# The attention-values product in four array quadrants, and one step order per engine, in a four-layer graph kernel

## The chip, the cores and the metric

The kernel runs on one core of one Trainium2 chip. The metric is the device time of one execution in microseconds (us), from launch to end. Five engines of the core take part, each with its own in-order instruction stream: PE (matrix multiplies, with PEld for the weight loads in front of them), DVE (vector engine), ACT (scalar engine), POOL (GpSimd) and SP (issues DMAs). They are kept in step by semaphores alone.

## The reference, cut to what matters

128 graphs of 64 nodes with 256 features pass four layers, each followed by a residual sum and a layer norm. The first layer is attention with 8 heads of 64; the change touches its last two products. The other three (mean aggregation, hypergraph convolution, gated similarity) matter as work that shares the engines.

```python
qkv = (x @ W_qkv).reshape(B, N, HEADS, 3, DIM_HEAD)
...
attn = jax.nn.softmax(dots, axis=-1) * LA
...
attn = attn + LG * adj + LD * jnp.exp(-dist)
out = jnp.einsum('bhij,bhjd->bhid', attn, v)
out = jnp.transpose(out, (0, 2, 1, 3)).reshape(B, N, HEADS * DIM_HEAD)
return out @ W_out + b_out
```

## The kernel before, in words

**Tiles and groups.** A tile is 128 rows, two graphs of 64 nodes. Four tiles (T) make a group, 16 groups (GRP) the whole input. Features are cut in 2 chunks of 128, the 512 inner columns in 4.

**Three groups in flight.** Line 305, `run`, walks one table, `SCHEDULE` (line 42), of (stream, step, index). Stream N is the next group (splitting its x in a high and a low part, its queries and first key chunk), A the group in layer 0, B the group before it in layers 1 to 3, C the group before that (its last scaling and its store). `rounds` (line 294) calls it for 19 rounds; 15 of them have both A and B, and 13 of these form the hardware loop. Every engine walks the same table and skips the steps it has no part in. So the table is the instruction order of PE, ACT, DVE and POOL alike. It also deals out the eight banks of PE's accumulation memory: lines 69 to 79 give banks 0 to 3 in turn to fills of N and A and banks 4 to 7 to those of B, in table order, and a fill waits (`emptied`, line 284) until the fill before it in its bank was read out.

**Precision.** Most products are three matmuls of a high and a low part (`product`, line 881). A step that feeds one is read out of its bank twice: by ACT, which writes the high part (`copy_out`, line 499), then by DVE, which writes what is left (`low_part`, line 598, the instruction at line 604). The next PE step waits for the low part.

**Scores** (`score`, line 938) are 64x64 products, one per head and graph, two tiles at a time. An instruction takes rows 0 to 63 or 64 to 127 of its operands, by the head's parity e, and writes partitions 0 to 63 or 64 to 127 of a bank, by the graph gr. Even heads write one bank and odd heads another. So four consecutive matmuls use the four combinations of input half and output half, called quadrants here.

**Values** (`pv`, line 973) take one tile per step. Head e = 0 or 1 of a pair is read from half e and written to half e of a single bank, so two of the four quadrants are used:

```python
for p in range(HP):
    for gr in range(2):
        for e in range(2):
            rows = slice(e * N, (e + 1) * N)
            ins = pe.matmul(dst[rows, p * P + gr * N:p * P + (gr + 1) * N], v[rows, i, gr, p, :],
                            pT[rows, i % 2, p, gr * N:(gr + 1) * N], start=True, stop=True,
```

ACT (line 522) and DVE (line 659) read that bank out into the parts of `oT`, which `out0` (line 995) multiplies with the output weights.

**Steps named below.** On PE: `q`, `k`, `v` projections (`proj`, 922; `val`, 931); `turnp` (964) transposes probabilities; `turn1`, `turn_h`, `turn3` (1003) transpose a layer's input; `graph_a` to `graph_d` and `graph_m` prepare the adjacency; `agg`, `spread`, `agg3` (`gathered`, 1058) apply it; `mean`, `up`, `down`, `hyper`, `qk`, `sim`, `out3` are products of layers 1 to 3. On DVE: `scale` (675, the instruction at 680) finishes a layer norm: `scale0`, `scale1`, `scale3`, and in `gated` (827), which also writes xg, the input of `turn3`. On POOL: `inv_root` (405) gives the factor that `scale` waits for; `residual` (396, step "mask") adds the bias to x; `split_low` (444) makes the low part of the next group's x. In this kernel `agg` waits for `turn1`'s low part, because it is given the bank that held it.

Of the kernel before, what the change touches and what calls it, by code (L numbers as in the profile page):

```python
# [13 lines left out]
ACT = mybir.ActivationFunctionType  # L14
# [6 lines left out]
P = 128  # L21
N = 64
D = 256
B = 128
H = 8
DH = 64
HID = 512
# [3 lines left out]
C = D // P  # L31
HP = H // 2
# [6 lines left out]

SCHEDULE = [
# [14 lines left out]
]  # L57

FILLS = {"graph_a": ["ht"], "graph_b": ["cnt"], "graph_c": ["sym"], "graph_m": ["meanT"], "graph_d": ["gT"],
# [6 lines left out]
_order = []  # L68
for _s, _n, _i in SCHEDULE:
    for _f in FILLS.get(_n, [_n]):  # L70
# [47 lines left out]
def graph_layers(nc, x, x_t, adj, adj_row0, mask_rows, wqkv, w_out, b_out, w_mean_t, w1_t, b1, gamma_c, beta_c, w2_t, b2,  # L118
                 wqk_t, bqk_c, wl_t, bl, wr_t, wd_r, bd_r, ident_c, ones3_c, mrow_c, out):
    with ExitStack() as ctx:  # L120
        def sb(name, shape, dt=F32):
            return ctx.enter_context(nc.sbuf_tensor(name, shape, dt))
# [47 lines left out]
        v = sb("v", [P, T, 2, HP, DH])  # L170
# [5 lines left out]
        pT = sb("pT", [P, 2, HP, P])  # L176
        oT = split("oT", [P, HP, 2 * P])
# [25 lines left out]
        agg3 = aggT  # L203
# [5 lines left out]
        gate = r[:, C:2 * C, :].rearrange("p a (b d) -> p (a b) d", d=D)  # L209
        xg = yw  # L210
        sim = hT0
# [45 lines left out]
        def count(sem, g, k, back=0):  # L257


            n = g * PER[sem] + (k - back * PER[sem])  # L260
            return (zero_ready, 4) if isinstance(n, int) and n <= 0 else (SEM[sem], n)

        def apart(eng, g):


            if not isinstance(g, int):
                eng.sem_inc(parted, 1)
# [7 lines left out]
        def bank_of(fill, i):  # L275
            return bank[BANK[(fill, i)][0]]
# [7 lines left out]
        def emptied(fill, i, g):  # L284

            b, (f, j), back = BEFORE[(fill, i)]
            if f in ("s_even", "s_odd"):
                return count("shift_ready", g, 2 * j + 1 + (f == "s_odd"), back)
            return count(READ_OUT[f], g, j + 1, back)

        def now_full(ins, fill, i):
            ins.then_inc(full[BANK[(fill, i)][0]], 1)

        def rounds(eng, body):

            body(0, None, None, None)
            body(1, 0, None, None)
            body(2, 1, 0, None)
            with eng.Fori(1, GRP - 2) as g:
                body(g + 2, g + 1, g, g - 1)  # L300
            body(None, GRP - 1, GRP - 2, GRP - 3)
            body(None, None, GRP - 1, GRP - 2)
            body(None, None, None, GRP - 1)

        def run(steps, n, a, b, c):
            group = {"N": n, "A": a, "B": b, "C": c}
            for stream, name, i in SCHEDULE:
                if group[stream] is not None and name in steps:
                    steps[name](group[stream], i)

# [77 lines left out]
        def _(pool):  # L388
# [80 lines left out]
                "out3": lambda g, i: inv_root(g, 3, "3", 2 * i, 2 * i + 2, i),  # L469
                "up": lambda g, i: inv_root(g, 4, "_h", i, i + 1, i),  # L470
            }
            rounds(pool, lambda n, a, b, c: run(steps, n, a, b, c))

        @block.scalar
        def _(act):
# [46 lines left out]
            def pv(g, i):  # L522
                act.wait_ge(*filled("oT", i, g))
                src = bank_of("oT", i)
                ins = act.activation(oT[0][:, :, (i % 2) * P:(i % 2 + 1) * P],  # L525
                                     src[:, :].rearrange("p (a n) -> p a n", a=HP), ACT.Copy)
                ins.then_inc(SEM["oT_hi"], 1)

            def graph_a(g, i):
# [31 lines left out]
                "turn_s": lambda g, i: copy_out(g, "turn_s", 0, flat(sT[:, :, :]), "sT_ready"),  # L561
                "agg3": lambda g, i: copy_out(g, "agg3", i, agg3[0][:, i, :], "agg3_hi"),
            }
            rounds(act, lambda n, a, b, c: run(steps, n, a, b, c))

        @block.vector
        def _(dve):
# [30 lines left out]
            def low_part(g, fill, i, lo, hi, name):  # L598

                dve.wait_ge(*count(f"{name}_hi", g, i + 1))  # L600
                src = bank_of(fill, i)[:, :]
                if len(lo.shape) == 3:
                    src = src.rearrange("p (a n) -> p a n", a=lo.shape[1])
                dve.tensor_tensor(lo, src, hi.bitcast(F32), ALU.subtract).then_inc(SEM[f"{name}_lo"], 1)  # L604
# [52 lines left out]
                    split_weight(wlr, raw_lr)  # L657

            def pv(g, i):
                at = slice((i % 2) * P, (i % 2 + 1) * P)  # L660
                low_part(g, "oT", i, oT[1][:, :, at], oT[0][:, :, at], "oT")
                if isinstance(g, int) and g == 0 and i < 2:
                    other_weights(i)

# [207 lines left out]
                "spread": low_chunk(spT, "spread", "spread"), "turn_h": low_chunk(hT, "turn_h", "hT"),  # L872
                "turn3": low_chunk(xgT, "turn3", "turn3"), "agg3": low_chunk(agg3, "agg3", "agg3"),
            }
            rounds(dve, lambda n, a, b, c: run(steps, n, a, b, c))

        @block.tensor
        def _(pe):
# [92 lines left out]
                now_full(ins, "pT", i)  # L971

            def pv(g, i):
                pe.wait_ge(*count("pT_ready", g, i + 1))
                pe.wait_ge(*count("v_ready", g, i + 1))
                pe.wait_ge(*emptied("oT", i, g))
                dst = bank_of("oT", i)
                apart(pe, g)
                for p in range(HP):
                    for gr in range(2):  # L980
                        for e in range(2):
                            rows = slice(e * N, (e + 1) * N)
                            ins = pe.matmul(dst[rows, p * P + gr * N:p * P + (gr + 1) * N], v[rows, i, gr, p, :],  # L983
                                            pT[rows, i % 2, p, gr * N:(gr + 1) * N], start=True, stop=True,
                                            skip_group_check=True)
                now_full(ins, "oT", i)

            def two_tiles(name, i, pairs_of, bias=None, ready=()):

# [163 lines left out]
                "turn3": lambda g, i: turned("turn3", g, i, xg, "xg_ready", 2),  # L1153
                "qk": qk, "sim": simi, "turn_s": turn_s, "agg3": agg3_, "out3": out3,
            }
            rounds(pe, lambda n, a, b, c: run(steps, n, a, b, c))


# [40 lines left out]
```

## Time and profile before

| | |
|---|---|
| device time, median of 3 runs | 1324.53 us (1323.3 to 1326.96) |
| profiled execution, device time | 1325.2 us |
| its span, first to last instruction | 1323.4 us |
| PE busy | 1238.9 us, 94% |
| DVE busy | 962.0 us, 73% |
| ACT, POOL busy | 551.2 us, 504.5 us |

The span is what the trace covers; 1.8 us of the execution lie outside it. "Busy" is the union of an engine's instruction records. A PE record lasts longer than the time after which the next can start, so several overlap: what a step costs is read from start to start, not from the length of a record. In the timeline a row gives start, length, instruction and count, and in brackets how long the engine was idle ahead of it and who ended that.

### The profile page before, as it was taken

How to read it: one execution, taken by the hardware profiler on the slowest of the kernel's cores; microseconds unless marked ns; L12 is line 12 of the kernel's file. 1: busy time of each engine (PE TensorE's matmuls, PEld its weight loads, DVE VectorE, ACT ScalarE, POOL GpSimd, SP SyncE). 2: the span in 40 equal slices, each digit the busy share in tenths (PEclk: the TensorE clock that was granted, in tenths of full speed). 3: DMA queues.
4: the chain of work that ended last, by engine and by line, in shares of the span. 5: the costliest groups of instructions: out<-in, count | busy, mean ns of one | idle time of the engine just before them, and what ended most of it. 6: DMA issues, size and time to landing. Idle time of an engine off the chain costs nothing.

```text
span 1323.4 us, 30705 instructions
## 1 busy us (share of the span) xinstructions
PE 1238.9 (94%) x11728; PEld 1073.7 (81%) x11728; DVE 962.0 (73%) x2115; ACT 551.2 (42%) x1058; POOL 504.5 (38%) x633
## 2 busy tenths in 40 slices
PE   5799999999999999999999999999999999999786
PEld 4688888788888888888788888878888887888665
DVE  5787776778767677776777777677876767787653
ACT  3335343543535344353444435354353435435221
POOL 2326252442624335262433525244262524425130
PEclk9799999999999999999999999999999999999897
DMA  6000101001010100101010010100101010010000
GB/s 204 21 21 17 42 2 41 16 20 36 0 54 2 40 16 20 36 0 44 12 40 16 20 36 0 40 16 20 36 16 40 0 40 20 0 37 2 21 1 16
DMA packets 43874, 34.93 MB, mean 26 GB/s; under 512 B 19320, under 2 KB 38718, under 8 KB 43839
## 3 DMA queue, kind: packets, MB, share of 16 engines
q1 hardware_dynamic: 43112, 34.04, 8.2%
q10 hardware_dynamic: 726, 0.40, 0.2%
q8 instruction: 24, 0.39, 0.1%
q14 instruction: 12, 0.09, 0.0%
HBM read 26.05 MB, written 8.39 MB: 26 GB/s over the span
## 4 chain that ended last, share of the span: by engine, by line
PE 72%; DVE 17%; issue 6%; ACT 3%; DMA 1%; POOL 0%; DVEq 0%; SPq 0%; POOLq 0%
PE bank L890 16%; PE bank L892 15%; PE bank L891 15%; PE bank L1066 6%; DVE x L680 5%; PE bank L1010 3%; PE bank L983 3%; PE bank L958 3%; DVE hT_lo L604 2%; PE bank L1124 2%; PE bank L886 2%; DVE yw L832 2%; DVE stats L669 1%; PE bank L948 1%; PE bank L1039 1%
## 5 line engine op out<-in xcount | busy, mean ns | idle before, releaser
L410 POOL TENSOR_SCALAR var<-mv 128x2 f32<-128x2 f32 (+1 forms) x192 | 43.4, 226 | 665.5 <-DVE mv L673 665.5
L680 DVE TENSOR_SCALAR x<-x,mv,rstd 128x256 f32<-128x256 f32 x256 | 158.3, 665 | 11.0 <-POOL rstd L413 11.0
L413 POOL TENSOR_TENSOR rstd<-var,negh 128x2 f32<-128x2 f32 (+1 forms) x192 | 130.4, 679 | 16.0
L502 ACT ACTIVATE qT<-bank 128x512 f32<-128x512 f32 x64 | 38.4, 600 | 217.9 <-PE bank L892 217.9
L604 DVE TENSOR_TENSOR hT_lo<-bank,hT_hi 128x512 fp32r<-128x512 f32 x160 | 105.3, 684 | 31.0 <-ACT hT_hi L502 30.7
L502 ACT ACTIVATE hT_hi<-bank 128x512 fp32r<-128x512 f32 x160 | 89.1, 604 | 52.8 <-PE bank L1066 46.0
L514 ACT ACTIVATE v<-bank 64x256 f32<-64x256 f32 x256 | 97.2, 380 | 17.5 <-PE bank L892 14.5
L669 DVE BATCH_NORM_STATS2 stats<-x 128x6 f32<-128x256 f32 x256 | 96.4, 419 | 4.4
L519 ACT ACTIVATE prob<-prob 128x512 f32<-128x512 f32 x64 | 40.5, 633 | 124.3 <-DVE prob L714 124.3
L525 ACT ACTIVATE oT_hi<-bank 128x512 fp32r<-128x512 f32 x64 | 38.2, 597 | 116.3 <-PE bank L983 116.3
L669 DVE BATCH_NORM_STATS2 stats<-r 128x6 f32<-128x512 f32 x64 | 44.4, 694 | 57.3 <-ACT r L502 57.3
L455 POOL TENSOR_TENSOR prob<-prob,srec 128x512 f32<-128x512 f32 x64 | 66.9, 1045 | 48.4 <-DVE srec L722 48.4
L460 POOL TENSOR_TENSOR prob<-prob,mix 128x512 f32<-128x512 f32 x64 | 82.2, 1285 | 6.1 <-POOL prob L455 2.1
L890 PE MATMUL bank<-w_hi,hT_hi 128*128 128x256 f32 x256 | 74.1, 289 | 0.2 <-DVE hT_lo L604 0.2
L890 PE MATMUL bank<-wo_hi,oT_hi 128*128 128x256 f32 x256 | 73.0, 285 | 0.5 <-DVE x L729 0.5
L890 PE MATMUL bank<-wm_hi,hT_hi 128*128 128x256 f32 x256 | 72.7, 284 | 0.0
L892 PE MATMUL bank<-wo_hi,oT_lo 128*128 128x256 f32 x256 | 71.5, 279 | 0.0
L891 PE MATMUL bank<-wo_lo,oT_hi 128*128 128x256 f32 x256 | 71.4, 279 | 0.0
L983 PEld LDWEIGHTS bank<-pT,v 64*64 64x64 f32 x2048 | 63.8, 137 | 9.4 <-issue 5.0
L892 PE MATMUL bank<-wm_hi,hT_lo 128*128 128x256 f32 x256 | 71.3, 279 | 0.0
L891 PE MATMUL bank<-wm_lo,hT_hi 128*128 128x256 f32 x256 | 71.3, 279 | 0.0
L891 PE MATMUL bank<-w_lo,hT_hi 128*128 128x256 f32 x256 | 71.1, 278 | 0.0
(206 smaller groups left out, 3864.1 us busy)
## 6 DMA issues: line engine op xcount, KB each, us to landing
xTin<-in_x_t SPq DMA_DIRECT2D x32, 256.0 KB, 2.8
xin<-in_x SPq DMA_DIRECT2D x16, 512.0 KB, 3.7
out_x<-x SPq DMA_DIRECT2D x32, 256.0 KB, 2.2
adjA<-in_adj SPq DMA_DIRECT2D x16, 128.0 KB, 2.5
adjB<-in_adj SPq DMA_DIRECT2D x32, 64.0 KB, 3.0
r<-in_wqkv SPq DMA_DIRECT2D x2, 512.0 KB, 8.9
x<-in_wqkv SPq DMA_DIRECT2D x1, 512.0 KB, 10.4
x<-in_w_out SPq DMA_DIRECT2D x1, 512.0 KB, 10.7
```

The lines of the kernel that those rows point to most:

```text
L413: pool.tensor_tensor(rstd[layer][:, lo:hi], var[layer][:, lo:hi], negh[:, lo:hi], ALU.pow).then_inc(SEM[f"rstd{n}"], 1)
L460: pool.tensor_tensor(u, u, mix[:, t:t + 2, :].rearrange("p t (a n) -> p t a n", a=1) .broadcast_to([P, 2, HP, N]), ALU.add).then_inc(SEM[" ...
L502: act.activation(dst, src[:, :], func, **kw).then_inc(SEM[ready], 1)
L514: ins = act.activation(v[e * N:(e + 1) * N, i, gr, :, :], src[gr * N:(gr + 1) * N, e], ACT.Copy)
L604: dve.tensor_tensor(lo, src, hi.bitcast(F32), ALU.subtract).then_inc(SEM[f"{name}_lo"], 1)
L669: dve.bn_stats(stats[layer][:, t, :], src[:, t, :]).then_inc(SEM[f"stats{n}"], 1)
L680: ins = dve.tensor_scalar(x[:, t, :], x[:, t, :], mv[layer][:, t, 0:1], rstd[layer][:, t:t + 1], ALU.subtract, ALU.mult)
L890: pe.matmul(out_ap, l[0], rr[0], start=(bias is None and j == 0), stop=False)
L891: pe.matmul(out_ap, l[0], rr[1], start=False, stop=False)
L892: ins = pe.matmul(out_ap, l[1], rr[0], start=False, stop=(j == len(pairs) - 1))
L983: ins = pe.matmul(dst[rows, p * P + gr * N:p * P + (gr + 1) * N], v[rows, i, gr, p, :], pT[rows, i % 2, p, gr * N:(gr + 1) * N], start=Tru ...
L1066: ins = pe.matmul(dst[:, t * P:(t + 1) * P], src[:, t, i * P:(i + 1) * P], mat[:, t, :], start=True, stop=True)
```

## The change

`pv` on PE does its work at even indices only, for two tiles i and i + 1 at once, and nothing at odd ones. Even head pairs (odd = 0) are written to halves e as before, in the bank of `oT` i. Odd head pairs (odd = 1) are written with the halves swapped, in the bank of `oT` i + 1. So a bank now holds half of the heads for both tiles; ACT and DVE write it to every second chunk of `oT`, and the output weights come with their rows permuted to fit. The number of matmuls stays. In place of the one table each engine walks its own order; the banks are dealt out by PE's. The stretches of the orders that matter are shown; between them steps stand much as before.

```diff
-SCHEDULE = [
-    ("A", "k", 1), ("B", "graph_a", 0), ("C", "scale3", 0), ("B", "turn1", 0), ("A", "mask", 0), ("B", "turn1", 1),
-    ("A", "k", 2), ("B", "graph_b", 0), ("B", "graph_m", 0), ("A", "k", 3), ("B", "agg", 0), ("A", "mixmat", 0),
-    ("B", "agg", 1), ("A", "score", 0), ("A", "shift", 0), ("B", "graph_c", 0), ("A", "shift", 1), ("B", "mean", 0),
-    ("B", "mean", 1), ("B", "graph_d", 0), ("A", "v", 0), ("B", "scale1", 0), ("A", "v", 1), ("A", "soft", 0),
...
-    ("A", "pv", 0), ("A", "pv", 1), ("B", "hyper", 1), ("A", "turnp", 2), ("A", "turnp", 3), ("B", "gated", 0),
-    ("A", "out0", 0), ("B", "gated", 1), ("N", "split_low", 0), ("N", "split", 0), ("A", "pv", 2), ("A", "pv", 3),
-    ("B", "turn3", 0), ("B", "turn3", 1), ("A", "norm0", 0), ("N", "q", 0), ("B", "qk", 0), ("B", "qk", 1),
...
+PE_ORDER = [
+    ("B", "turn1", 0), ("B", "turn1", 1), ("A", "k", 1), ("B", "graph_a", 0), ("A", "k", 2), ("B", "graph_m", 0),
+    ("B", "graph_b", 0), ("A", "k", 3), ("A", "mixmat", 0), ("B", "agg", 0), ("B", "agg", 1), ("B", "graph_c", 0),
+    ("A", "score", 0), ("B", "mean", 0), ("B", "mean", 1), ("B", "graph_d", 0), ("A", "v", 0), ("A", "v", 1),
+    ("A", "v", 2), ("B", "spread", 0), ("B", "spread", 1), ("A", "v", 3), ("B", "up", 0), ("B", "up", 1),
...
+    ("A", "score", 1), ("A", "turnp", 0), ("B", "down", 0), ("B", "down", 1), ("A", "turnp", 1), ("B", "hyper", 0),
+    ("A", "pv", 0), ("B", "hyper", 1), ("A", "turnp", 2), ("A", "turnp", 3), ("A", "pv", 1), ("A", "out0", 0),
+    ("A", "pv", 2), ("B", "turn3", 0), ("B", "turn3", 1), ("N", "q", 0), ("B", "qk", 0), ("A", "pv", 3),
...
+ACT_ORDER = [
+    ("B", "turn1", 0), ("B", "turn1", 1), ("A", "k", 1), ("B", "graph_a", 0), ("B", "graph_m", 0), ("A", "mixmat", 0),
+    ("A", "k", 2), ("B", "agg", 0), ("A", "k", 3), ("B", "agg", 1), ("A", "shift", 0), ("A", "v", 0),
+    ("B", "graph_d", 0), ("A", "v", 1), ("B", "spread", 0), ("B", "spread", 1), ("A", "shift", 1), ("N", "split", 0),
...
+DVE_ORDER = [
+    ("B", "graph_a", 0), ("B", "turn1", 0), ("B", "turn1", 1), ("A", "mask", 0), ("C", "scale3", 0),
+    ("B", "graph_b", 0), ("B", "agg", 0), ("B", "agg", 1), ("B", "graph_c", 0), ("A", "mixmat", 0), ("A", "shift", 0),
+    ("B", "mean", 0), ("B", "mean", 1), ("B", "scale1", 0), ("A", "shift", 1), ("B", "spread", 0), ("B", "spread", 1),
...
+POOL_ORDER = [
+    ("B", "graph_a", 0), ("B", "graph_b", 0), ("B", "mean", 0), ("A", "mask", 0), ("B", "mean", 1), ("A", "soft", 0),
...
+    ("A", "soft", 2), ("A", "soft", 3), ("N", "split_low", 0), ("B", "hyper", 0), ("B", "hyper", 1),
...
@@ ACT @@
-                ins = act.activation(oT[0][:, :, (i % 2) * P:(i % 2 + 1) * P],
-                                     src[:, :].rearrange("p (a n) -> p a n", a=HP), ACT.Copy)
+                ins = act.activation(oT[0][:, i % 2:HP:2, :], src[:, :].rearrange("p (a n) -> p a n", a=HP // 2), ACT.Copy)
@@ DVE @@
-                low_part(g, "oT", i, oT[1][:, :, at], oT[0][:, :, at], "oT")
+                low_part(g, "oT", i, oT[1][:, i % 2:HP:2, :], oT[0][:, i % 2:HP:2, :], "oT")
@@ PE @@
             def pv(g, i):
+                if i % 2:
+                    return
+                pe.wait_ge(*count("pT_ready", g, i + 2))
+                pe.wait_ge(*count("v_ready", g, i + 2))
+                for odd in range(2):
+                    pe.wait_ge(*emptied("oT", i + odd, g))
+                    apart(pe, g)
+                ins = [None, None]
+                for k in range(2):
+                    for pair in range(HP // 2):
+                        for gr in range(2):
+                            for odd in range(2):
+                                p = 2 * pair + odd
+                                col = (pair * 2 + k) * P + gr * N
+                                for e in range(2):
+                                    rows, to = slice(e * N, (e + 1) * N), (e + odd) % 2
+                                    ins[odd] = pe.matmul(bank_of("oT", i + odd)[to * N:(to + 1) * N, col:col + N],
+                                                         v[rows, i + k, gr, p, :], pT[rows, k, p, gr * N:(gr + 1) * N],
+                                                         start=True, stop=True, skip_group_check=True)
+                for odd in range(2):
+                    now_full(ins[odd], "oT", i + odd)
```

## Rows read from the trace of the kernel before

**Rows 1.** The page: span; busy time and share by engine; the chain's shares.

```profile
span 1323.4 us, 30705 instructions
PE 1238.9 (94%) x11728; PEld 1073.7 (81%) x11728; DVE 962.0 (73%) x2115; ACT 551.2 (42%) x1058; POOL 504.5 (38%) x633
PE 72%; DVE 17%; issue 6%; ACT 3%; DMA 1%; POOL 0%; DVEq 0%; SPq 0%; POOLq 0%
```

**Rows 2.** Stretches of the span: length, busy time of PE, PEld, DVE, ACT, POOL; clock.

```profile
0.00:51.00 51.00, 29.04 (x292) 23.09 (x292) 28.48 (x43) 20.73 (x41) 18.77 (x22) 0.89 0.44 133
598.30:676.60 78.30, 75.99 (x736) 66.07 (x733) 58.50 (x130) 34.30 (x66) 31.36 (x40) 1.00 0.08 23
1223.20:1290.80 67.60, 52.83 (x354) 45.70 (x353) 41.34 (x104) 16.09 (x28) 17.56 (x28) 0.91 0.04 11
```

**Rows 3.** Groups of PE by line: records, busy us, mean ns, idle before.

```profile
L983 PE MATMUL bank<-pT,v 64*64 64x64 f32 x2048 | 68.2, 222 | 2.0 <-ACT pT L502 2.0
L958 PE MATMUL bank<-kT,qT 64*64 64x64 f32 x2048 | 37.2, 221 | 0.0
```

**Rows 4.** PE's timeline, around the scores and values of one round.

```profile
658.96 1.16 PE L958 MATMUL bank<-kT,qT 64*64 64x64 f32 x64
660.05 0.66 PE L969 MATMUL bank<-ident,prob 128*128 128x128 f32 x4
...
667.66 2.08 PE L983 MATMUL bank<-pT,v 64*64 64x64 f32 x64
669.67 0.28 PE L1107 MATMUL bank<-bias,ones 96*128 96x256 bf16 x1
```

**Rows 5.** PE's timeline, the same round: the first steps, and where PE waits.

```profile
621.88 0.40 PE L890 MATMUL bank<-xT_hi,wq_hi 128*128 128x512 f32 x1
...
629.19 0.40 PE L892 MATMUL bank<-xT_hi,wk_lo 128*128 128x512 f32 x1
630.59 1.13 PE L1066 MATMUL bank<-meanT,x 128*128 128x128 f32 x8 [1.00 <-DVE hT_lo L604]
631.65 0.28 PE L908 MATMUL bank<-mj,mi 4*128 4x64 bf16 x4
632.11 1.13 PE L1066 MATMUL bank<-meanT,x 128*128 128x128 f32 x8 [0.17 <-DVE hT_lo L604]
...
656.86 1.64 PE L1010 MATMUL bank<-ident,r 128*128 128x128 f32 x13 [0.36 <-ACT r L502]
...
676.55 0.44 PE L1010 MATMUL bank<-ident,yw 128*128 128x128 f32 x2
677.52 0.87 PE L1010 MATMUL bank<-ident,yw 128*128 128x128 f32 x6 [0.53 <-DVE yw L832]
```

**Rows 6.** DVE's timeline at the start of the round.

```profile
625.50 0.18 DVE L749 RECIPROCAL rdeg<-degm 128x4 f32<-128x4 f32 x1
625.63 4.22 DVE L680 TENSOR_SCALAR x<-x,mv,rstd 128x256 f32<-128x256 f32 x4
629.77 0.68 DVE L604 TENSOR_TENSOR hT_lo<-bank,hT_hi 128x512 fp32r<-128x512 f32 x1
```

**Rows 7.** POOL's timeline beside it, a root, and its splitting later on.

```profile
626.93 2.44 POOL L401 TENSOR_TENSOR xin<-xin,bout 128x1024 f32<-128x1024 f32 x1
...
643.96 0.71 POOL L413 TENSOR_TENSOR rstd<-var,negh 128x2 f32<-128x2 f32 x1
...
674.02 2.57 POOL L448 TENSOR_TENSOR xT_lo<-xTin,xT_hi 128x512 fp32r<-128x512 f32 x2
```

**Rows 8.** DVE's timeline: two scalings with POOL idle, two beside POOL's splitting.

```profile
643.38 0.70 DVE L680 TENSOR_SCALAR x<-x,mv,rstd 128x256 f32<-128x256 f32 x2
...
674.09 2.65 DVE L680 TENSOR_SCALAR x<-x,mv,rstd 128x256 f32<-128x256 f32 x2
```

**Rows 9.** ACT's read-outs of one bank, by line.

```profile
L525 ACT ACTIVATE oT_hi<-bank 128x512 fp32r<-128x512 f32 x64 | 38.2, 597 | 116.3 <-PE bank L983 116.3
L514 ACT ACTIVATE v<-bank 64x256 f32<-64x256 f32 x256 | 97.2, 380 | 17.5 <-PE bank L892 14.5
```

More of the change, by code:

```diff
@@ L37 @@
 BIG = 2.0 ** 120
-SCHEDULE = [
[14 rows of a table removed]
-]
+PE_ORDER = [
[10 rows of a table added]
+]
+ACT_ORDER = [
[9 rows of a table added]
+]
+DVE_ORDER = [
[10 rows of a table added]
+]
+POOL_ORDER = [
[4 rows of a table added]
+]
+ORDERS = {"pe": PE_ORDER, "act": ACT_ORDER, "dve": DVE_ORDER, "pool": POOL_ORDER}
+SCHEDULE = PE_ORDER
 FILLS = {"graph_a": ["ht"], "graph_b": ["cnt"], "graph_c": ["sym"], "graph_m": ["meanT"], "graph_d": ["gT"],
@@ L303, in rounds, with run @@
             body(None, None, None, GRP - 1)
-        def run(steps, n, a, b, c):
+        def run(order, steps, n, a, b, c):
             group = {"N": n, "A": a, "B": b, "C": c}
-            for stream, name, i in SCHEDULE:
+            for stream, name, i in order:
                 if group[stream] is not None and name in steps:
@@ L471, in _ @@
             }
-            rounds(pool, lambda n, a, b, c: run(steps, n, a, b, c))
+            rounds(pool, lambda n, a, b, c: run(POOL_ORDER, steps, n, a, b, c))
         @block.scalar
@@ L563, in _ @@
             }
-            rounds(act, lambda n, a, b, c: run(steps, n, a, b, c))
+            rounds(act, lambda n, a, b, c: run(ACT_ORDER, steps, n, a, b, c))
         @block.vector
@@ L659, in pv @@
             def pv(g, i):
-                at = slice((i % 2) * P, (i % 2 + 1) * P)
-                low_part(g, "oT", i, oT[1][:, :, at], oT[0][:, :, at], "oT")
+                low_part(g, "oT", i, oT[1][:, i % 2:HP:2, :], oT[0][:, i % 2:HP:2, :], "oT")
                 if isinstance(g, int) and g == 0 and i < 2:
@@ L874, in _ @@
             }
-            rounds(dve, lambda n, a, b, c: run(steps, n, a, b, c))
+            rounds(dve, lambda n, a, b, c: run(DVE_ORDER, steps, n, a, b, c))
         @block.tensor
@@ L973, in pv @@
             def pv(g, i):
[L974 to L986, printed above, removed]
+                if i % 2:
[19 more added lines that the diff above has]
+                    now_full(ins[odd], "oT", i + odd)
             def two_tiles(name, i, pairs_of, bias=None, ready=()):
@@ L1155, in _ @@
             }
-            rounds(pe, lambda n, a, b, c: run(steps, n, a, b, c))
+            rounds(pe, lambda n, a, b, c: run(PE_ORDER, steps, n, a, b, c))
 def kernel(**inputs):
@@ L1180 @@
         "adj_row0": a["adj"][:, 0, :].reshape(B // 2, P).T, "mask_rows": _np.concatenate([rows, cols], axis=2).reshape(4, -1),
-        "wqkv": _np.moveaxis(a["L0_gnn_W_qkv"].reshape(D, H, 3, DH), 2, 0).reshape(3, D, H * DH), "w_out": a["L0_gnn_W_out"], "b_out": a["L0_gnn_b_out"],
+        "wqkv": _np.moveaxis(a["L0_gnn_W_qkv"].reshape(D, H, 3, DH), 2, 0).reshape(3, D, H * DH), "w_out": a["L0_gnn_W_out"].reshape(HP, 2, DH, D)[_np.arange(HP)[:, None], _np.array([[0, 1], [1, 0]] * (HP // 2))].reshape(HID, D), "b_out": a["L0_gnn_b_out"],
         "w_mean_t": a["L1_gnn_W"].T, "w1_t": a["L2_gnn_W1"].T, "b1": a["L2_gnn_b1"],
```

25 rows, old and new, of tables (ACT_ORDER, DVE_ORDER, PE_ORDER, POOL_ORDER) are left out of this document.

## The prediction

> **What bounds the kernel now.** I read the page first, then the stretches of the span, then PE's timeline through one round, and DVE's and POOL's beside it where PE waits. PE is busy for 1238.9 of 1323.4 us and carries 72% of the chain that ended last, DVE 17% [rows 1]. A round of the steady state takes 78.30 us, with PE busy for 75.99, its clock at the full level (share 1.00, so 2.4 GHz) and DVE busy for 58.50 [rows 2]. So in the 15 rounds that hold both A and B, PE's own work and PE's waits are nearly all of the time, and whatever is taken from PE shortens the round, as long as the step that PE meets next is ready that much earlier too. Only the start (29.04 us of PE in 51.00) and the last round with B alone (52.83 in 67.60) are held by other things [rows 2].
>
> Two places stand out. First, the values product: 2048 records take 68.2 us, while the scores product, with as many records of the same 64x64 shape, takes 37.2 [rows 3]. Second, PE's waits inside a round [rows 5]: about 1.0 us of idle time before `agg` 0, 0.17 before `agg` 1, 0.36 in `turn_h`, 0.53 in `turn3`. They understate the loss, since a record's length covers some of it, so I take them from start to start below.
>
> **Part 1, the values in four quadrants.** From the start of the 64 records of two tiles to the next step it is 669.67 - 667.66 = 2.01 us; the 64 records of one scores step take 660.05 - 658.96 = 1.09 us [rows 4]. Scores alternate over four quadrants, values over two. The new `pv` issues the same 64 records per two tiles, with four different quadrants in any four matmuls in turn, and two matmuls that share an output half write different banks, as in scores. I price it at the scores' pace: 2.01 - 1.09 = 0.92 us a pair, 32 pairs, 29.4 us of PE. The bounds are 0 (the pace stays) and 29.4; I know no reason for more than the scores' pace. I take 28, because the first group's two pairs lie in the start, where PE is idle for over 40% and DVE's preparation of weights sets the pace [rows 2].
>
> What comes with it. The two banks now become full together 1.1 us after the start instead of at 1.0 and 2.0. ACT's read-out is 597 ns a bank [rows 9] and DVE's some 0.68, as the same kind of row for `hT_lo` shows [rows 6], and these are as large as before; the two-piece target of 256 columns each costs nothing that I can see, bounded by one more short instruction overhead, hidden while PE runs `hyper` and `turnp`. But the low part of tile 1 is ready only about 1.1 + 0.6 + 0.6 + 0.7 = 3.0 us and a wait behind `hyper` 0's statistics after `pv` began, and PE has `hyper` 1 (670.8 - 669.7) and two `turnp` between, some 2.0 us of work after `pv`'s 1.1. I expect `out0` 0 to wait 0.25 us per round. The permuted output weights are an input: free. `pv` needs both tiles' probabilities at once, which in the old order were due one step later; PE's order has `turnp` 1 and `hyper` 0 in front, so that is covered.
>
> **Part 2, one order per engine.** The stall before `agg`: the last record of `k` 3 starts at 629.19 and would be followed after 0.24 by `agg` 0, which starts at 630.59: 1.16 us lost. The four short `mixmat` matmuls begin at 631.65 and `agg` 1 at 632.11, about 0.28 more than they need. Together 1.44 us [rows 5]. Its cause: `agg` waits for DVE to read `turn1` out, and DVE does this only from 629.77, behind the four scalings of `scale3`, which began at 625.63 and took 4.22 us [rows 6]. They are that slow because POOL's `residual`, 2.44 us, runs beside them [rows 7]; two scalings take 0.70 us with POOL idle and 2.65 beside POOL's work [rows 8]. The change puts `turn1` first on PE and ACT, and DVE reads it out straight after `graph_a` (done at 625.7), so both low parts exist by about 627.0. It puts `residual` on POOL behind `mean` 0. PE does q 3 from 621.88 [rows 5], then `turn1`, and reaches `agg` 0 at about 629.7. The next thing to be late is `meanT` out of ACT, at about 628.7, and `bhT` out of POOL for `graph_c`, at about 630.9 against PE's 631.5. (These clock times, and those below, are estimates: I laid each engine's steps end to end in the new order, at the lengths they have in this round, and let each wait for what it needs; the frame is this round's clock.). So I let all 1.44 us go. `scale3`, now behind, takes some 1.4 us with POOL free; it delays `graph_b` on DVE to about 631.2, and its store lands some microseconds before `mean` 0 needs it.
>
> `residual` moved: on POOL it now stands in front of `mean` 1's root, for 2.44 us [rows 7]. I get the root of `mean` 0 at 640.3, `residual` to 642.7, the root of `mean` 1 (0.71 and a short addition ahead of it [rows 7]) at 643.7, both scalings of x2 done at about 644.45, against PE reaching `spread` at 644.5. So it costs nothing and has nothing to spare. On ACT `v` 0's read-out, 4 x 0.38 = 1.5 us [rows 9], stands before `graph_d`'s: done at 644.05, also just in time.
>
> `split_low` moved: before, it ran on POOL (2.57 us from 674.02 [rows 7]) while DVE scaled for `gated` 1, which took 2.65 instead of 0.70 [rows 8], and `turn3` started its second half at 677.52 instead of about 676.8, 0.7 us lost [rows 5]. Now it runs before `hyper`'s roots: POOL is free at about 669.3, `hyper` 1's root comes at 671.8, xg is whole at 673.6, and PE, 0.9 x 2 + 1.6 us earlier than before, is there at about 673.3. I keep 0.35 us of stall, so 0.35 is won. The wait in `turn_h` (0.5 us, for the fourth tile of `up` to leave its bank) stays, since nothing stands between; so does the one in `out3`, for the same reason.
>
> Sum per round: 1.44 + 0.35 + 0.15 (short refills that go with the waits) - 0.25 = 1.7 us, in 15 rounds 25 us, and 1 us for the rounds at the end, which have waits of the same kind: 26. Bounds: below, nothing or a loss (a rival); above, all the waits of a round, 78.30 - 75.99 = 2.3 us idle and about as much hidden in the records, 4.5 x 15 = 67.
>
> **The sum** is made against the profiled execution: 1325.2 - 28 - 26 = 1271 us. The median of the runs, 1324.5, is 0.7 lower; I leave 1271.
>
> **Rivals.** (a) The values keep their pace. The scores' matmuls from the lower input half write one bank and those from the upper half the other; the values' two halves always shared one bank [rows 4]. It may be this sharing, and not the number of quadrants, that makes the values slow. The new code still lets both halves write each bank. Then part 1 is 0, or worse than nothing for `out0`, whose wait grows less than 0.3 us, and the time is 1325.2 - 26 = 1299. Against it: the values run at half the scores' pace, just what two quadrants against four would give if each had its own pace. The Trainium skill (TensorEngine Tiling, Gotcha 1: PSUM Pressure) says that different row tiles cannot access one bank at the same time. By that rule this rival holds; no row before shows four quadrants with shared banks.
>
> (b) The orders win nothing net: each stall removed returns at the next late step, of which I found three with under 0.1 us to spare. Then 1325.2 - 28 = 1297. For it: that closeness. Against: the 1.44 us before `agg` have a plain cause that goes.
>
> (c) Slower than before. One mechanism: POOL work beside DVE's scalings, moved onto the path. If `residual` overlaps `scale1`'s four scalings as it did `scale3`'s, these take 4.22 instead of 1.4, and `spread`, which has no slack, starts 2.8 us later; if `split_low` still overlaps `gated`'s, that is 1.95 more: 4.8 us a round. It decides from the 3.5 us a round that the change saves (1.84 + 1.7). At 4.8 the round is 1.3 longer: 1325.2 + 15 x 1.3 = 1345. Against it: `residual` should be over when the second pair is scaled.
>
> (d) More is won than I see: the separate orders hide the refills and the waits in `turn_h` and `out3` too, another 1.2 us a round: 1253.
>
> **Chances.** Forecast 0.60 (1257 to 1285); (a) 0.12; (b) 0.14; (c) 0.04; (d) 0.08; both parts fail, about no change, 0.02. The range takes in the forecast, (a) and (b): 1255 to 1300. A measurement of this kernel can tell about 0.3% from no change, 4 us. Faster 0.94, same 0.02, slower 0.04.
>
> **What would show it.** In the profile after: the group of the values product near 37 us for 2048 records, and 1.1 us from its start to the next step; were (a) true, 2.0. No idle time before `agg` ended by a low part, `scale3`'s four scalings near 1.4 us. `spread` starting without a wait for x; a wait there of over 1 us would be (c). A short wait of `out0` for oT_lo. A round of 74.7 us with PE busy for some 73.5. I am wrong if a round takes under 73.7 or over 75.7, whichever part it comes from.

## The result, and the profile after

The kernel after takes 1269.38 us (median of 4 runs, 1268.96 to 1272.89) against 1325.27 us for the one before in the same comparison (4 runs, 1323.3 to 1326.96): ratio 0.9582, 95% interval 0.9563 to 0.9602, so 56 us less. The forecast was 1271.0. The profiled execution of the kernel after is the longest of its four, 1272.89 us; its span is 1271.1, 52.3 less than before [rows 1].

The page, with the lines of [rows 1]: span; busy time and share of each engine; the chain's shares by engine.

```profile
span 1271.1 us, 30705 instructions
PE 1208.7 (95%) x11728; PEld 1050.0 (83%) x11728; DVE 907.0 (71%) x2115; ACT 539.2 (42%) x1058; POOL 500.5 (39%) x633
PE 91%; DVE 4%; ACT 2%; DMA 1%; issue 1%; POOL 0%; SPq 0%; POOLq 0%; DVEq 0%
```

The number of instructions is as it was. PE has lost 30.2 us of busy time, just what the group of the values product lost (68.2 to 38.0, below). DVE has lost 55 us for the same 2115 instructions, and its share of the chain fell from 17% to 4%: PE hardly waits for it any more.

Two stretches, columns as in [rows 2]: a steady round, and the round with B alone.

```profile
573.20:647.70 74.50, 73.89 (x741) 64.43 (x733) 54.80 (x130) 33.49 (x66) 31.03 (x39) 1.00 0.08 25
1168.60:1238.60 70.00, 55.31 (x360) 48.42 (x352) 41.10 (x105) 16.60 (x29) 17.19 (x28) 0.88 0.04 11
```

A round, from one start of `turn3` to the next, is 647.67 - 573.24 = 74.43 us, 3.8 less than before, with PE busy for 73.9 at the full clock. From the start of the first `turn3` to that of the last (14 rounds) the span is 51.7 us shorter, the start before it 2.9. The round with B alone is 2.4 us *longer* than before, at a clock of 0.88 against 0.91, and the end is as before: 51.7 + 2.9 - 2.4 + 0.1 = 52.3. That round varies with the clock: over the profiled executions of all kernels of this document it lies between 66.6 us at a clock of 0.95 and 70.5 at 0.88, and a kernel that differs from the one after only in the order of two loops has 68.0 at 0.92.

The groups of scores and values, as in [rows 3]:

```profile
L1015 PE MATMUL bank<-pT,v 64*64 64x64 f32 x2048 | 38.0, 224 | 0.8 <-ACT pT L528 0.8
L982 PE MATMUL bank<-kT,qT 64*64 64x64 f32 x2048 | 37.2, 221 | 0.0
```

The values now run at the scores' pace, and the mean record is as long as before (224 ns against 222): more of them overlap. PE's timeline through that round, for [rows 4, 5] (573.24 and 647.67 are the two starts of `turn3`):

```profile
573.24 1.23 PE L1043 MATMUL bank<-ident,yw 128*128 128x128 f32 x8
...
603.95 0.29 PE L932 MATMUL bank<-mj,mi 4*128 4x64 bf16 x4
604.17 2.05 PE L1099 MATMUL bank<-meanT,x 128*128 128x128 f32 x16
606.05 1.06 PE L1072 MATMUL bank<-bhT,hT 128*128 128x128 f32 x8
...
618.88 1.95 PE L1099 MATMUL bank<-gT,x 128*128 128x128 f32 x16
...
629.44 1.64 PE L1043 MATMUL bank<-ident,r 128*128 128x128 f32 x13 [0.36 <-ACT r L528]
...
640.41 1.16 PE L1015 MATMUL bank<-pT,v 64*64 64x64 f32 x64
641.50 0.28 PE L1140 MATMUL bank<-bias,ones 96*128 96x256 bf16 x1
...
647.67 1.23 PE L1043 MATMUL bank<-ident,yw 128*128 128x128 f32 x8
```

`agg` 0 and 1 are one run of 16 with no idle time ahead (604.17), where there were two runs with waits of 1.00 and 0.17. The values take 641.50 - 640.41 = 1.09 us. `turn3` is one run of 8 without the 0.53 in the middle. `turn_h` keeps its 0.36. By start-to-start times, before against after: `k` 3 up to the next step 2.64 and 1.59; `agg` with `mixmat` 2.57 and 2.11; the values 2 x 2.01 and 2 x 1.09; `turn3` 1.59 and 0.98; `up`'s first tile 1.81 and 1.64; `turnp` ahead of `out0` 0.79 and 0.97 (the new wait of `out0`). Together they make some 3.9 us, against the 3.8 from round to round.

DVE's and POOL's timelines at the places of [rows 6, 7, 8], one fence each:

```profile
599.94 1.29 DVE L629 TENSOR_TENSOR hT_lo<-bank,hT_hi 128x512 fp32r<-128x512 f32 x2
601.15 0.73 DVE L711 SCALAR_TENSOR_TENSOR mi<-masks,mcst 4x512 bf16<-4x512 uint8 x1
...
602.07 1.36 DVE L704 TENSOR_SCALAR x<-x,mv,rstd 128x256 f32<-128x256 f32 x4
...
616.17 1.40 DVE L704 TENSOR_SCALAR x<-x,mv,rstd 128x256 f32<-128x256 f32 x2
618.17 0.74 DVE L704 TENSOR_SCALAR x<-x,mv,rstd 128x256 f32<-128x256 f32 x2 [0.60 <-POOL rstd L439]
...
642.25 1.28 DVE L629 TENSOR_TENSOR oT_lo<-bank,oT_hi 128x512 fp32r<-128x512 f32 x2
```

```profile
614.70 2.40 POOL L427 TENSOR_TENSOR xin<-xin,bout 128x1024 f32<-128x1024 f32 x1
617.40 0.73 POOL L439 TENSOR_TENSOR rstd<-var,negh 128x2 f32<-128x2 f32 x1
...
641.20 2.51 POOL L474 TENSOR_TENSOR xT_lo<-xTin,xT_hi 128x512 fp32r<-128x512 f32 x2
```

`scale3` (602.07) takes 1.36 us where it took 4.22. `residual` (614.70) holds up `scale1`'s first pair (1.40 for two instead of 0.70), the second pair ends at 618.9, and `spread`, which starts at 618.88 and needs that pair from its third matmul on, does not wait: in time, with almost nothing to spare. `split_low` now runs at 641.20, beside DVE's read-outs of banks, and these take their usual 0.64 us each.

### The profile page after: what moved, and what is told of

It is laid out like the page before. It is cut to its first block, busy times and chain, and to the rows that moved or that the text cites. A ratio compares the mean times of both kernels' runs of the same rounds, so it can differ in the third digit from the quotient of the medians.

```text
span 1271.1 us, 30705 instructions
## 1 busy us (share of the span) xinstructions
PE 1208.7 (95%) x11728; PEld 1050.0 (83%) x11728; DVE 907.0 (71%) x2115; ACT 539.2 (42%) x1058; POOL 500.5 (39%) x633
## 4 chain that ended last, share of the span: by engine, by line
PE 91%; DVE 4%; ACT 2%; DMA 1%; issue 1%; POOL 0%; SPq 0%; POOLq 0%; DVEq 0%
PE bank L914 21%; PE bank L915 19%; PE bank L916 19%; PE bank L1099 7%; PE bank L1043 4%; PE bank L1015 3%; PE bank L982 3%; PE bank L1157 2%; PE bank L993 2%; PE bank L1141 2%; PE bank L910 2%; PE bank L972 1%; PE bank L1072 1%; DVE hT_lo L629 1%; ACT r L528 1%; PE bank L1165 1%
## 5 line engine op out<-in xcount | busy, mean ns | idle before, releaser
L540 ACT ACTIVATE v<-bank 64x256 f32<-64x256 f32 x256 | 96.3, 376 | 74.7 <-PE bank L916 72.4
L704 DVE TENSOR_SCALAR x<-x,mv,rstd 128x256 f32<-128x256 f32 x256 | 101.6, 442 | 16.2 <-POOL rstd L439 16.2
L916 PE MATMUL bank<-w_hi,hT_lo 128*128 128x256 f32 x256 | 71.9, 281 | 0.0
L528 ACT ACTIVATE spT_hi<-bank 128x512 fp32r<-128x512 f32 x64 | 36.6, 597 | 81.7 <-PE bank L1043 71.6
```

Source lines behind the costliest of these rows:

```text
L528: act.activation(dst, src[:, :], func, **kw).then_inc(SEM[ready], 1)
L540: ins = act.activation(v[e * N:(e + 1) * N, i, gr, :, :], src[gr * N:(gr + 1) * N, e], ACT.Copy)
L704: ins = dve.tensor_scalar(x[:, t, :], x[:, t, :], mv[layer][:, t, 0:1], rstd[layer][:, t:t + 1], ALU.subtract, ALU.mult)
L916: ins = pe.matmul(out_ap, l[1], rr[0], start=False, stop=(j == len(pairs) - 1))
```

## The experiments

Every ratio is to runs of the kernel before on the same chip. The totals agree with the forecast; what was open is whether its parts do.

**Each part alone.** First the values alone: the new `pv`, read-outs and weights in the kernel before, with its one table.

> The kernel before with the new values product, its permuted weights and its read-outs, and the one table of before. Theory (two parts that add up): the pair of tiles takes 1.09 us in place of 2.01, and the time falls by 26 to 29 us, to 1296 to 1299; the waits before agg stay. Rival (the two parts need each other, the shorter product only lengthens the wait of turn3 or out0): under 15 us, 1310 or more.

Measured: 1328.81 us (10 runs), ratio 1.0029 (1.0018 to 1.004). Nothing is won; it is a little slower. The product itself is not at fault. Its group, and PE's timeline at `turn3` in two consecutive rounds:

```profile
L989 PE MATMUL bank<-pT,v 64*64 64x64 f32 x2048 | 38.0, 224 | 2.5 <-ACT pT L502 2.5
```

```profile
675.59 0.44 PE L1017 MATMUL bank<-ident,yw 128*128 128x128 f32 x2
677.85 0.88 PE L1017 MATMUL bank<-ident,yw 128*128 128x128 f32 x6 [1.82 <-DVE yw L830]
...
755.89 1.54 PE L1017 MATMUL bank<-ident,yw 128*128 128x128 f32 x6 [1.83 <-DVE yw L830]
757.66 0.63 PE L889 MATMUL bank<-xT_lo,wq_hi 128*128 128x512 f32 x1
```

PE arrives earlier and waits 1.82 us for xg where it waited 0.53. DVE's timeline there, then POOL's:

```profile
668.44 0.69 DVE L819 SCALAR_TENSOR_TENSOR x<-x,bank 128x512 f32<-128x512 f32 x1 [0.23 <-PE bank L1115]
...
674.43 2.63 DVE L678 TENSOR_SCALAR x<-x,mv,rstd 128x256 f32<-128x256 f32 x2
677.10 0.69 DVE L830 SCALAR_TENSOR_TENSOR yw<-r,x 128x512 f32<-128x512 f32 x1
```

```profile
674.36 2.56 POOL L448 TENSOR_TENSOR xT_lo<-xTin,xT_hi 128x512 fp32r<-128x512 f32 x2
```

The second half of xg comes from `gated` 1, whose two scalings take 2.63 us beside `split_low`. That chain starts from `hyper` 0, ahead of the values: from its first sum (668.44) to xg (677.79) DVE has no idle time, 9.35 us where the same steps took 9.69 in the kernel before. So the shorter `pv` gains that 0.34 and otherwise only makes PE wait at the chain's end. The wait costs a second time too. In the next round the same six transposes take 1.54 us instead of 0.88, and a matmul of 512 columns 0.63 where [rows 5] has 0.40. The stretches of 6.4 us from the two `turn3` on (columns as in [rows 2]) have the clock at 1.00 and at 0.73, so part of the second ran at the lower level, 1.2 GHz:

```profile
675.60:682.00 6.40, 4.58 (x27) 3.72 (x24) 6.22 (x12) 3.22 (x6) 1.32 (x2) 1.00 0.34 103
753.60:760.00 6.40, 4.57 (x24) 3.76 (x17) 5.96 (x10) 2.52 (x5) 1.36 (x2) 0.73 0.33 103
```

A round is 77.8 us without such a fall and 79.4 with it, against 78.2. Six of the 14 rounds have it, which makes some 9 us; without it, as an estimate, this kernel would be some 5 us faster than the one before, 0.4 a round of the 1.84.

Then the orders alone: the kernel after with the old `pv`.

> The changed kernel with the values product of before, its two steps next to each other in PE's order. Theory: 74.4 + 1.84 = 76.3 us a round and 1297 to 1299 in all, so the orders alone bring 26 to 29. Rival (the orders suit only the shorter product): over 1305.

Measured: 1295.10 us (4 runs), ratio 0.9769 (0.9753 to 0.9785): 30 us for the orders. So the values bring 1295.1 - 1269.4 = 26 us on top of the orders, and nothing without them. In the two profiled executions it is less: the rounds are 75.7 and 74.4 us, 1.3 apart, 18 us over the 14. Of the 1.84 us a round, 0.18 goes to the new wait of `out0` and 0.13 to `turn3`, which takes 0.98 instead of the 0.85 it takes here; the rest stays open.

**What in the orders the values need.** The suspect was `split_low`'s place. In the kernel before with the new values, one move in the one table:

```diff
-    ("A", "turnp", 0), ("B", "down", 0), ("A", "turnp", 1), ("A", "soft", 3), ("B", "down", 1), ("B", "hyper", 0),
+    ("A", "turnp", 0), ("B", "down", 0), ("A", "turnp", 1), ("A", "soft", 3), ("N", "split", 0), ("N", "split_low", 0),
+    ("B", "down", 1), ("B", "hyper", 0),
...
-    ("A", "out0", 0), ("B", "gated", 1), ("N", "split_low", 0), ("N", "split", 0), ("A", "pv", 2), ("A", "pv", 3),
+    ("A", "out0", 0), ("B", "gated", 1), ("A", "pv", 2), ("A", "pv", 3),
```

> The kernel before with the new values product and, in its one table, split and split_low moved ahead of down 1, so that POOL splits before hyper's roots. Theory (the values alone brought nothing because xg came late behind POOL's splitting, and the clock fell in that wait): turn3's wait goes, 0.7 + 1.84 us a round: 1285 to 1292, no steady round at the lower clock. Rival (another wait ends last after the values, out0 or hyper): 1305 or more.

Measured: 1296.65 us (4 runs), ratio 0.9798 (0.9782 to 0.9814). Its timelines at that place, of DVE, POOL and PE:

```profile
507.06 0.73 DVE L679 TENSOR_SCALAR x<-x,mv,rstd 128x256 f32<-128x256 f32 x2
```

```profile
501.91 2.52 POOL L449 TENSOR_TENSOR xT_lo<-xTin,xT_hi 128x512 fp32r<-128x512 f32 x2
```

```profile
508.24 1.20 PE L1018 MATMUL bank<-ident,yw 128*128 128x128 f32 x8
...
511.01 0.47 PE L889 MATMUL bank<-spT_hi,wqk_hi 128*128 128x512 f32 x1 [0.16 <-DVE spT_lo L604]
```

The scalings are at 0.73, `turn3` does not wait, and no steady round shows the lower clock. At least five of the microseconds expected are missing. The same move with the old values:

> The kernel before with split and split_low moved in its one table as in the run before, the values product untouched. Theory: only turn3's 0.7 us a round goes, 8 to 12 us, 1313 to 1317. Rival (POOL's roots now come too late for gated 0): no faster than 1322.

Measured: 1315.56 us (4 runs), ratio 0.9946 (0.9928 to 0.9964). Between these two kernels the values bring 18.9 us, 1.2 of their 1.84 us a round. Three new waits take the rest, start to start: 0.17 ahead of `out0`, 0.11 in `turn3`, and 0.3 ahead of `qk` (511.01), because ACT and DVE read out the two banks of values, which now become full together, before those of `turn3`. So the two edits make a square: neither 1, new values alone 1.0029, the move alone 0.9946, both 0.9798. Alone they are worth +0.3% and -0.5%, together -2.0%: the values' saving is there only when `split_low` is out of the way. (Of the +0.3%, the rounds at the lower clock make some 0.7.)

The reverse, in the kernel after, only POOL's order changed:

```diff
-    ("A", "soft", 2), ("A", "soft", 3), ("N", "split_low", 0), ("B", "hyper", 0), ("B", "hyper", 1),
+    ("A", "soft", 2), ("A", "soft", 3), ("B", "hyper", 0), ("B", "hyper", 1), ("N", "split_low", 0),
```

> The changed kernel with split_low on POOL back behind hyper's roots. Theory: gated 1 is scaled beside it again, 2.65 us in place of 0.73, and turn3's second half waits some 0.7 to 1.5 us in each of 14 rounds: 10 to 20 us slower, 1279 to 1289. Rival (the wait is hidden now): within 3 us of 1269.

Measured: 1312.51 us (4 runs), ratio 0.9897 (0.9873 to 0.992): 43 us over the kernel after, more than expected. PE's timeline at `turn3` in two rounds:

```profile
593.78 0.88 PE L1043 MATMUL bank<-ident,yw 128*128 128x128 f32 x6 [1.81 <-DVE yw L856]
...
670.11 1.07 PE L1043 MATMUL bank<-ident,yw 128*128 128x128 f32 x6 [1.81 <-DVE yw L856]
```

The wait of 1.81 us is back, and in 10 of the 14 rounds the clock falls behind it (0.86 over the 12.1 us from 667.90). Rounds are 76.3 us without such a fall and 77.9 with it, against 74.4: some 27 of the 43 us are the wait, some 16 the clock.

**The stall before `agg`.** My cause was `scale3` in front of `agg`'s read-outs, slowed by `residual`. In the kernel before, `scale3` moved behind `turn1` 1:

```diff
-    ("A", "k", 1), ("B", "graph_a", 0), ("C", "scale3", 0), ("B", "turn1", 0), ("A", "mask", 0), ("B", "turn1", 1),
+    ("A", "k", 1), ("B", "graph_a", 0), ("B", "turn1", 0), ("A", "mask", 0), ("B", "turn1", 1), ("C", "scale3", 0),
```

> The kernel before with one entry of its one table moved: scale3 behind both turn1 steps, which concerns DVE alone. Theory (agg waits for turn1's low part behind scale3): both waits before agg go, at most 1.44 us in 15 rounds, 22 us; 18 to 22, so 1303 to 1307. Rival (scale3 only blocks something else then, graph_b or the masks, or POOL's residual still slows it): under 8 us.

Measured: 1318.13 us (4 runs), ratio 0.9944 (0.9923 to 0.9966), 7 us where I expected some 20. DVE's, POOL's and PE's timelines:

```profile
623.91 2.28 DVE L687 SCALAR_TENSOR_TENSOR mi<-masks,mcst 4x512 bf16<-4x512 uint8 x1
...
626.98 1.36 DVE L680 TENSOR_SCALAR x<-x,mv,rstd 128x256 f32<-128x256 f32 x4
```

```profile
623.25 2.40 POOL L401 TENSOR_TENSOR xin<-xin,bout 128x1024 f32<-128x1024 f32 x1
```

```profile
627.20 1.13 PE L1066 MATMUL bank<-meanT,x 128*128 128x128 f32 x8 [0.18 <-DVE hT_lo L604]
...
632.62 0.38 PE L890 MATMUL bank<-wm_hi,hT_hi 128*128 128x256 f32 x1 [0.52 <-DVE hT_lo L604]
```

The 1.00 before `agg` is down to 0.18, but the delay moved twice: `residual` now meets the mask operation (2.28 us instead of 0.73), and `mean` waits 0.52 for a read-out that stands behind `scale3`. So `residual`'s place was the next suspect. It goes back in its old place, in the kernel after:

```diff
-    ("B", "graph_a", 0), ("B", "graph_b", 0), ("B", "mean", 0), ("A", "mask", 0), ("B", "mean", 1), ("A", "soft", 0),
+    ("B", "graph_a", 0), ("A", "mask", 0), ("B", "graph_b", 0), ("B", "mean", 0), ("B", "mean", 1), ("A", "soft", 0),
```

> The changed kernel with residual on POOL back behind graph_a. Theory: scale3 is slow again (some 3 to 4 us in place of 1.36) and bhT and graph_b come later, so graph_c may wait, 0 to 1.5 us a round: 0 to 20 us slower. Rival (its move was free and brought nothing): within 3 us of 1269; or faster by the slack that scale1 wins.

Measured: 1286.44 us (4 runs), ratio 0.9716 (0.9693 to 0.9739), 17 us over the kernel after. The size is as expected, the place is not: `scale3` stays at 1.36, and the operation that `residual` meets is `mj`, 0.33 us in the kernel after. `residual` itself takes 2.87 us instead of 2.40; it began beside a `mi` that had begun 0.12 us earlier and took its usual 0.73. The timelines of DVE, POOL and PE:

```profile
607.60 0.73 DVE L711 SCALAR_TENSOR_TENSOR mi<-masks,mcst 4x512 bf16<-4x512 uint8 x1
608.26 2.48 DVE L715 TENSOR_SCALAR mj<-masks,mcst 4x256 bf16<-4x256 uint8 x1
```

```profile
607.72 2.87 POOL L427 TENSOR_TENSOR xin<-xin,bout 128x1024 f32<-128x1024 f32 x1
```

```profile
610.98 0.27 PE L932 MATMUL bank<-mj,mi 4*128 4x64 bf16 x4 [0.51 <-DVE mj L715]
...
613.49 1.16 PE L1072 MATMUL bank<-bhT,hT 128*128 128x128 f32 x8 [0.26 <-POOL bhT L455]
```

**How much is POOL's order alone?** The values and `split_low` early in the one table, as above, and POOL alone walks its new order (which also has `soft` 1 behind `up` 0); PE, ACT and DVE keep the table.

> The kernel of the run e10 (new values product, split and split_low early in the one table), with POOL alone walking the changed kernel's POOL order, in which residual also stands behind mean 0; PE, ACT and DVE keep the one table. Theory (scale3, ahead of turn1's low part, is slow only because residual runs beside it): scale3 takes 1.4 us in place of 4.2, both waits before agg go, about 1.4 us a round, and the time is 1274 to 1280. Rival (DVE's and PE's own orders are needed, because the work ahead of the low part stays): 1288 or more.

Measured: 1280.17 us (5 runs), ratio 0.9644 (0.9631 to 0.9658). So `split_low` and POOL's order with the values give about 47 of the 56 us, and the own orders of PE, ACT and DVE the last 9 or so (8 by the ratios, 11 by the times of two chips).

**A wait that stayed.** `q` 3 in front of `out3`, to cover its 0.43 us for `agg3`'s low part:

```diff
-    ("N", "k", 0), ("B", "agg3", 0), ("B", "agg3", 1), ("B", "out3", 0), ("B", "out3", 1), ("N", "q", 3),
+    ("N", "k", 0), ("B", "agg3", 0), ("B", "agg3", 1), ("N", "q", 3), ("B", "out3", 0), ("B", "out3", 1),
```

> The changed kernel with q 3 moved in PE's order from behind out3 to in front of it. Theory: it fills the 0.43 us in which out3 waits for agg3's low part, and the next round's start has slack: 0.3 to 0.45 us a round, 5 to 7 us faster, 1263. Rival (the wait comes back at graph_a, whose edges DVE now writes a step later against PE, or at agg for meanT): within 2 us of 1269.

Measured: 1277.04 us (5 runs), ratio 0.9649 (0.9636 to 0.9662): 8 us slower than the kernel after, as the rival had it. PE's timeline:

```profile
527.44 0.40 PE L1051 MATMUL bank<-identb,edge 128*128 128x128 bf16 x4 [0.40 <-DVE edge L768]
...
529.74 0.65 PE L1080 MATMUL bank<-ident,meanA 128*128 128x128 f32 x4 [0.46 <-POOL meanA L447]
```

The wait in `out3` is gone, and two longer ones (0.40 and 0.46 us of idle time, against 0.24) stand before the next round's graph steps, which `q` 3 had covered. A round takes 75.1 us instead of 74.4.

**What sets the values' pace.** Two quadrants, but each input half to a bank of its own, over two tiles (it mixes up halves of the two tiles' outputs; the work is the same):

```diff
-                    for pair in range(HP // 2):
+                    for p in range(HP):
                         for gr in range(2):
-                            for odd in range(2):
...
+                            for e in range(2):
+                                rows, b = slice(e * N, (e + 1) * N), (e + k) % 2
+                                ins[b] = pe.matmul(bank_of("oT", i + b)[rows, p * P + gr * N:p * P + (gr + 1) * N],
```

> The changed kernel, with the values product in two quadrants again, but the two input halves of consecutive matmuls always write different banks; each bank then holds one half of each of two tiles, so the first layer's output mixes up the tiles' halves. Theory (the number of quadrants sets the pace): 2.01 us for two tiles, the group near 67 us, some 1298 in all. Rival (it was the shared bank): 1.09 us and 1269.

Measured: 1296.54 us (one run). Its group:

```profile
L1012 PE MATMUL bank<-pT,v 64*64 64x64 f32 x2048 | 68.2, 222 | 0.8 <-ACT pT L528 0.8
```

68.2, as with one bank: with two quadrants, sharing a bank costs nothing, and it is the number of quadrants that costs. Then all four quadrants, but eight matmuls in two of them before eight in the other two:

```diff
-                    for pair in range(HP // 2):
-                        for gr in range(2):
-                            for odd in range(2):
+                    for odd in range(2):
+                        for pair in range(HP // 2):
+                            for gr in range(2):
```

> The changed kernel with the loop over even and odd head pairs outside the loops over pairs and graphs: all four quadrants are used, but eight matmuls in turn alternate between two of them before the other two follow. Theory (PE starts matmuls in order, so only neighbours overlap): 2.0 us a pair of tiles, some 1298. Rival (matmuls further back in the queue start early when their quadrant is free, or the mere use of four is what counts): 1.1 us and 1269.

```profile
L1015 PE MATMUL bank<-pT,v 64*64 64x64 f32 x2048 | 51.1, 227 | 0.8 <-ACT pT L528 0.8
```

Measured: 1278.26 us (one run), the group between the two others at 51.1, which neither side had. And the four quadrants with two neighbours from the same input half:

```diff
-                            for odd in range(2):
...
-                                for e in range(2):
+                            for e in range(2):
+                                for odd in range(2):
```

> The changed kernel with the two innermost loops of the values product swapped: still four quadrants in any four matmuls, but two neighbours now read the same input half and write different output halves and banks. Theory (four quadrants in flight are enough): 1.09 us a pair of tiles, 1269. Rival (a weight load overlaps the matmul ahead only when it goes to the other input half, as the Trainium skill says in TensorE: Matmul & The Clock Gate, Part 3): between 1.1 and 2.0 us, clearly above 1.3, and 1275 to 1298.

```profile
L1015 PE MATMUL bank<-pT,v 64*64 64x64 f32 x2048 | 38.0, 224 | 0.8 <-ACT pT L528 0.8
```

Measured: 1271.31 us (one run), at full pace. The Trainium skill (TensorE: Matmul & The Clock Gate, Part 3: Packing small matmuls — row/col tiling) has it that a weight load overlaps matmuls in flight only when its row group differs; here every second pair of neighbours shares one, and the pace is the same, so this kernel does not bear the rule out. What the full pace and this order have in common is that any four in a row use four quadrants.

## Why the prediction was right, and where its steps were not

**The total and the round.** 1271 forecast, 1269.4 measured; a round of 74.7 forecast with PE busy for 73.5, measured 74.43 and 73.9. The group near 37 us is 38.0, `scale3` near 1.4 is 1.36, no wait before `agg`, `spread` just in time, a new wait of 0.2 ahead of `out0` (0.25 forecast), `turn_h` and `out3` waiting as before. The orders alone brought 30 us (26 forecast), the values on top 26 by the medians (28 forecast) and 18 in the profiled executions. Part of the closeness is luck: the 14 rounds won 3.7 us each, more than the 1.84 + 1.7 of the sum, the start won 2.9, for which hardly anything was counted, and the round with B alone lost 2.4, where 1 was to be won.

**Rival (a)** falls twice: the kernel after lets both halves write each bank and runs at 38.0 us, and two quadrants with separate banks stay at 68.2. The rule of the Trainium skill that it leaned on (TensorEngine Tiling, Gotcha 1: PSUM Pressure), that different row tiles cannot access one bank at the same time, is not borne out by these two numbers. In the kernels before and after, the two input halves write different partitions of the bank they share; no run has them write the same ones.

**What failed: the two parts as separate terms.** The sum took 0.92 us x 32 for part 1, whatever part 2 did; by it the values alone should give 1297, which is also rival (b)'s figure. They give 1328.81. The total held all the same, because the new place of `split_low` had been laid out with both savings in it. My first paragraph had the condition: what is taken from PE shortens the round "as long as the step that PE meets next is ready that much earlier too". I did not apply it to part 1. `turn3` already waited 0.53 us for xg [rows 5], so xg, not PE, set the time at that point, and the two pairs of values stand in front of it. A saving of 1.84 us ahead of a step that is already late is worth little before that step's own chain gets shorter: 0.4 us, and less than nothing with the clock that fell. Rival (b) failed in the same way, since it let the orders win nothing and still kept the values' 28.

**`split_low`'s move, priced at 0.35 us a round,** 5 us in all. With the old values it is worth 7 us, near the price. With the new ones it is worth 43 in the kernel after (undone) and about 30 in the kernel before (1.0029 against 0.9798). The difference is the values' saving, which it releases, and the lower clock that follows PE's wait of 1.8 us in some rounds. I had also kept 0.35 us of stall in `turn3`; 0.13 is left (0.98, against the 0.85 of the orders with the old values).

**The stall before `agg`** was priced right (1.44 us a round; 1.05 + 0.46 measured), and its cause named too narrowly. That `scale3` stood in the way was the smaller part: with `scale3` moved, only 7 us came. `residual` lengthens whichever of `scale3`, `mi` or `mj` it meets, and all of them lie ahead of a step that PE needs. "It costs nothing and has nothing to spare" was said of `residual`'s new place, and holds. Its old place costs 17 us, most of the 1.44 x 15 = 22 priced for this stall; `scale3`'s old place is worth no more than the 7.

**Rival (c)** was right in its mechanism and small in its size: `residual` does meet `scale1`'s first pair, for 0.70 us more, which a later wait for the root hides. Rival (d)'s gain in `turn_h` and `out3` did not come, and the one try at `out3` moved the wait elsewhere.

**Left open:** why eight matmuls in two quadrants, then eight in the other two, run at 51.1 us and not at 68.2; why the clock falls in some rounds and not in others with the same wait; whether the 2.4 us of the round with B alone come from the change or from the clock. No version tried beats the kernel after.

## What to carry to other kernels

Before a saving on the busiest engine is counted, look at the next step on it that waits: a saving ahead of it is worth only as much as that step's own chain can be shortened, so two edits that are worth +0.3% and -0.5% apart can be worth -2% together, and each should be tried alone. When one long GpSimd instruction slows DVE, moving what it hit only lets it hit the next one; put the GpSimd instruction where DVE reads banks. For 64x64 products, deal consecutive matmuls over all four quadrants; which half goes to which bank did not matter here.

## What the runs showed of the hardware that I had not expected

**POOL and DVE.** A DVE instruction that works only in SBUF can wait for nearly the whole of a POOL instruction: `mj` took 2.48 us instead of 0.33 beside a `residual` of 2.4 us, `mi` 2.28 instead of 0.73, two scalings 2.63 instead of 0.70. Others are not touched: in the kernel after, `oT_lo`'s two read-outs of a bank (642.25) take 1.28 us in the middle of `split_low`, and two statistics of x (615.16), with one operand in SBUF, their usual 0.76 in the middle of `residual`. Where DVE had begun first, `residual` took longer (2.87 us, above). The Trainium skill (SBUF — State Buffer, Who interferes with whom) has the rule: DVE shares a pair of ports with GpSimd, and an instruction in a 2-port mode or with two SBUF inputs uses it, so one of the two waits until the other is through. These rows agree, though none shows the mode itself. The amount depends on the POOL instruction that is met: with only POOL's order changed, `scale3`'s four scalings took 2.14 us beside the `meanA` of 1.04 us. DVE's timeline of that kernel, then POOL's:

```profile
605.14 2.14 DVE L687 TENSOR_SCALAR x<-x,mv,rstd 128x256 f32<-128x256 f32 x4
```

```profile
605.45 1.04 POOL L430 TENSOR_TENSOR meanA<-adjB,rdeg 128x512 f32<-128x512 f32 x1 [0.70 <-DVE rdeg L756]
```

**The clock.** A PE wait of 1.8 us in a steady round was followed, in 6 of 14 rounds of one kernel and 10 of 14 of another, by a stretch with a granted clock below full (0.73 over 6.4 us, 0.86 over 12.1 us). In the first of these, transposes took 1.75 times as long and a 512-column matmul 1.6 times; such rounds took 79.4 us instead of 77.8. In the other kernels, whose longest PE wait in the steady rounds is the 1.0 us before `agg`, all of these rounds are at 1.00.

**Order of quadrants.** 2048 small matmuls took 38.0, 51.1 or 68.2 us by the order and choice of quadrants alone, with a mean record of 222 to 227 ns in all three: the length of a record says nothing of the pace here, only the time from start to start does.
